# Reordering reciprocals, routed rows' normalisation and spare products in a one-core decoder layer

## What is computed

```
x = layernorm(x + attn(x))            # sparse attention: each token picks 96 of its keys by top-k
x = layernorm(x + retention(x, ctx))  # 16 heads, decaying causal mask
x = layernorm(x + moe(x))             # 8 experts, 2 chosen per token, gates from a softmax
```

## Time and profile before

| | us |
|---|---|
| median of three executions | 669.03 |
| the three | 668.65, 669.03, 680.7 |
| the profiled execution | 668.53 |
| its span, first to last instruction | 666.7 |

### The profile page before, as it was taken

How to read it: one execution, slowest core, us unless ns; L and a number is a source line. 1 busy time by engine, 2 the same in 40 slices (tenths; PEclk the granted TensorE clock), 3 DMA queues, 4 the chain that set the end, 5 groups by cost and what they waited for, 6 DMA issues and landing times.

```text
span 666.7 us, 22154 instructions
## 1 busy us (share of the span) xinstructions
PE 585.0 (88%) x8225; PEld 439.7 (66%) x8225; DVE 432.2 (65%) x1618; ACT 406.9 (61%) x1381; POOL 268.0 (40%) x428
## 2 busy tenths in 40 slices
PE   5478988998898699999999898989997997789996
PEld 4244664665566367867787577757775677778886
DVE  0938848865976777578657976478657775333653
ACT  4437756674776657668765676377755665445352
POOL 1413912911570497017502898219304652005310
PEclk9869999999999969999999899799999999799999
DMA  5030153122014051543353435344262623886551
GB/s 170 2 123 14 28 189 133 22 63 84 19 24 137 14 162 27 188 157 108 107 156 117 130 80 174 99 154 116 66 206 77 189 67 100 242 241 196 166 160 44
DMA packets 58594, 75.86 MB, mean 114 GB/s; under 512 B 14256, under 2 KB 47480, under 8 KB 57336
## 3 DMA queue, kind: packets, MB, share of 16 engines
q1 hardware_dynamic: 56952, 71.30, 35.8%
q0 software_dynamic: 1536, 3.15, 1.6%
HBM read 58.92 MB, written 8.62 MB: 101 GB/s over the span
## 4 chain that ended last, share of the span: by engine, by line
PE 34%; POOL 11%; issue 9%; ACT 6%; DVE 4%; DMA 1%; SPq 0%; DVEq 0%; POOLq 0%; ACTq 0%
PE bW L1364 4%; PE bH L1299 3%; PE bR L1314 3%; PE bG L1083 3%; PE bM L920 3%; POOL gb L852 3%; PE bH L1350 2%; PE bG L1350 2%; ACT qV L1567 2%; PE bS L1102 2%; PE bM L1130 1%; PE bR L1222 1%; PE bM L1125 1%; POOL sorted_tokens L864 1%; POOL acc L895 1%
## 5 line engine op out<-in xcount | busy, mean ns | idle before, releaser
L1515 ACT ACTIVATE ppn<-pp,rls 128x224 f32<-128x224 f32 (+1 forms) x128 | 59.0, 461 | 34.0 <-DVE rls L1815 33.7
L1833 DVE TENSOR_TENSOR gs<-bG,rank_t 96x512 f32<-96x512 f32 x96 | 65.5, 682 | 15.0 <-PE bG L1083 13.8
L1507 ACT ACTIVATE pp<-pp,nmx 128x224 f32<-128x224 f32 x96 | 46.5, 484 | 31.1 <-DVE nmx L1826 30.2
L1896 DVE TENSOR_TENSOR sm<-bC,cst 128x512 f32<-128x512 f32 x64 | 43.6, 681 | 23.0 <-PE bC L1239 23.0
L1083 PE MATMUL bG<-oh,kspl 128*96 128x512 f32 x160 | 56.6, 435 | 0.0
L810 POOL TENSOR_TENSOR r<-x,cst 128x256 f32<-128x256 f32 x8 | 5.8, 725 | 123.0 <-DVE x L1860 123.0
L1826 DVE CUSTOM_DVE_ANT_0 pp<-bS,cst 128x224 f32<-128x224 f32 x96 | 36.3, 378 | 27.3 <-PE bS L1102 27.2
L1599 ACT ACTIVATE ht<-bH,wt 128x128 f32<-128x128 f32 x156 | 44.4, 370 | 14.5 <-PE bH L1299 14.5
L920 PE MATMUL bM<-cst,ppn 128*128 128x128 f32 (+1 forms) x224 | 47.8, 284 | 5.5 <-ACT ppn L1515 5.3
L1525 ACT COPY pts<-bM 128x256 f32<-128x256 f32 x96 | 35.4, 369 | 27.2 <-PE bM L920 26.3
L1299 PE MATMUL bH<-xt,wt 128*128 128x128 f32 x312 | 43.5, 284 | 3.0 <-DVE xt L2025 3.0
(11 more groups left out here) (296 smaller groups left out, 1644.8 us busy)
## 6 DMA issues: line engine op xcount, KB each, us to landing
wt<-in_experts SPq DMA_DIRECT2D x61, 578.0 KB, 4.0
sidx<-far_slots SPq DMA_DIRECT2D x8, 1536.0 KB, 6.9
vstk<-gs SPq DMA_DIRECT2D x96, 64.0 KB
xs<-sorted_tokens SPq DMA_DIRECT2D x45, 64.0 KB, 3.9
expert_rows<-ot SPq DMA_DIRECT2D x45, 64.0 KB, 3.7
sorted_tokens<-acc SPq DMA_DIRECT2D x9, 256.0 KB, 2.9
cst<-shape_constants SPq DMA_DIRECT2D x1, 1595.5 KB, 6.3
xn<-in_x SPq DMA_DIRECT2D x8, 128.0 KB, 3.3
```

What stands on the lines that cost most here:

```text
L1507: AC(pp[:, s % 2, 0:w], bS[:, 0:w] if s < T0 else pp[:, s % 2, :], ACT.Exp, scale=1.0 if s < T0 else -1.0, bias=nmx[:, s % 2:s % 2 + 1], a ...
L1515: AC(ppn[:, t % 2, 0:w], pp[:, t % 2, 0:w], ACT.Copy, scale=rls[:, t % 2:t % 2 + 1]).then_inc(s_nrm.sem, 1)
L1833: TT(gs[:, g % 2, :].rearrange("p (t j) -> p t j", j=FAR), bG[0:96, :].rearrange("p (t j) -> p t j", j=FAR), rank_t[:, :].rearrange("p (o ...
L1896: free(TT(sm[:, u % 4, :].rearrange("p (v c) -> p v c", v=4), bC[:, :].rearrange("p (v c) -> p v c", v=4), C("causal").rearrange("p (o c) ...
```

## The change

It has three parts.

1. VectorE's reciprocal of tiles 3 to 15 moves from s+0.75 to s+0.25, ahead of the one-hot rows and of whatever stage C has at s+0.5. Tiles 0 to 2 keep their place. ScalarE's order is not touched.
2. The parts of the routed rows of batches 0 to 3 come earlier, by other tables. `collect` of the second batch of each group moves from slot 10 to 9, `summed` from slots 11 and 14 to 10 and 12, `means` from 14 and 17 to 13 and 15, and `normed` from 16 and 19 to 14 and 16.
3. Batch 0 has fewer fills: one product in slot 0 and one in slot 2 in place of two each in slots 0, 1 and 2. The other batches keep theirs (38 products in all before, 34 after).

```diff
+FILLS_FIRST, FILLS = 1, 2
 FETCH_SLOTS = (4, 5, 6)
-SUM_LATE, MEAN_LATE, NORM_LATE = 4, 7, 9
+SUM_LATE, MEAN_LATE, NORM_LATE = 3, 6, 7
...
             step, s = ends[g]
-            s += 2 + 3 * (n - GROUPS[g][0][0])
+            s += 2 + 2 * (n - GROUPS[g][0][0])
...
-                    if s in FILLED[i.n <= GROUPS[0][0][-1] + 1]:
-                        fill(2)
+                    if s in FILLED[0 < i.n <= GROUPS[0][0][-1] + 1]:
+                        fill(FILLS_FIRST if i.first else FILLS)
...
                     if s == 0:
-                        fill(2)
+                        fill(FILLS_FIRST if i.first else FILLS)
...
+            def inverse(i, t):
+
+                dve.wait_ge(s_exp.sem, s_exp.at(i.n, t + 1))
+                nc.vector.reciprocal(rls[:, t % 2:t % 2 + 1], lsum[:, t % 2:t % 2 + 1]).then_inc(s_rec.sem, 1)
+
             def stage_b(s, i):
                 p = i.par
                 if s < 0:
                     return
+                if s == int(s) + 0.25 and T0 - 1 <= s < NT:
+                    inverse(i, int(s))
                 if s in (1.25, 3.25, 5.25, 7.25, 9.25, 11.25):
...
-                if s == int(s) + 0.75 and s < NT:
-
-                    t = int(s)
-                    dve.wait_ge(s_exp.sem, s_exp.at(i.n, t + 1))
-                    nc.vector.reciprocal(rls[:, t % 2:t % 2 + 1], lsum[:, t % 2:t % 2 + 1]).then_inc(s_rec.sem, 1)
+                if s == int(s) + 0.75 and s < T0 - 1:
+                    inverse(i, int(s))
```

## The result

Side by side on one chip the changed kernel takes 675.27 us (median of 4, 672.37 to 677.1) against 668.84 before: a ratio of 1.011, with a 95% interval of 1.006 to 1.016. One of the four executions before, at 680.7 us, was a slow one and is left out of the ratio. The forecast was 667.2 us with a range of 660 to 673.5. The changed kernel is slower by 1%, under the 2% that I took as what a measurement can tell, but clear of its interval, and outside the range.

A forecast was written before the change was run, and what follows sets the result against it. TensorE, busy 88%, was taken as the bound, so edits count where it idles. Terms +5.9 - 5.0 + 0.7 - 2.5 = -0.9 us on 668.5 gave 667.6, stated as 667.2 us; own range 664 to 671, overall 660 to 673.5.

The forecast's parts named there:

- Part 1: Earlier reciprocals: VectorE's stands in slots 3, 7 and 15, less a gain, net +5.9 us, at most 8.3.
- waits for `ppn`: TensorE's waits, 5.3 us in all, mostly tile 2's: 1.2 us to be gained at tiles 5, 9 and 12.
- Slot 3: VectorE stands 0.98 us, some 0.35 returns a slot later: about 0.65 in five batches, 3.2 us.
- Slots 7 and 15: Slot 7: 0.46 us in batches 1, 2, 3, 5, total 1.8; slot 15: 0.75 in batches 0 to 2, total 2.1.
- VectorE's waits for the exponential: Sign for the reciprocals: VectorE's waits for ScalarE's exponential, called small now, rise to some 15 us.
- Part 2, step 7 to 8: Start of step 8: first product 3.4 us earlier, clock 1.6 us more; sum -5.0, ends -3.4 and -6.1.
- Part 2, step 5: End of step 5: late `acc` and `rkn` delay +2.0, `rqn` wait of 1.28 goes; net +0.7, ends -1.3 and +5.
- Part 3: Batch 0: fewer fills give 4.5 us at most, a later grant rise costs 2.0; net -2.5, ends -4.5 and +5.2.
- rival 3: Batch 0: the clock stays low without the fills, +5.2 us there; time 675.3 us; chance 0.10.
- rival 2: Slots 3, 7, 15 of every batch: VectorE's stands not given back, 8.3 to 12.7 us; 671 to 674.4 us; chance 0.14.
- Rival 1: The earlier reciprocals cost nothing; time 659.7, or 658.6 with the clock's whole share, taken as 660 us; chance 0.24.
- rival 4: Step 8's start: weights' load and `xt` late for another reason, other parts cancel, nothing reaches the end; 668.5 us; chance 0.08.

The follow-up runs named there:

- the control: The kernel before, unchanged, run and profiled again on the chip where other runs were made: ratio 1.0015 (0.998 to 1.005).
- tile 3 alone: The kernel before with only tile 3's reciprocal moved early, tables and fills as before: ratio 1.011 (1.007 to 1.016).
- the new tables alone: The kernel before with only the routed rows' parts earlier, reciprocals and fills as before: ratio 0.9915 (0.989 to 0.994), again 0.9935 (0.990 to 0.997).
- run of step 7 alone: The kernel before with the routed rows' parts earlier for batches 2 and 3 only: ratio 0.992 (0.988 to 0.995).

## Why the prediction was wrong

**Part 1, the step that failed.** The prediction had +5.9 us with an upper end of 8.3; the trace shows +17.3 in stage B. The upper end was itself mis-added: without the 1.2 us of waits for `ppn` the stands sum to 7.1, and the 1.2 was added once more. The trace's figure is one pair of executions; three things make up the difference to the forecast.

- *The term that was not in the sum: the clock.* I priced each stand at full clock and took the sum of stands for the price. Taking every quarter where the grant was 1.00, from this trace or, where it fell, from one of the others, the stands come to 8.4 us: batch 0 0.9, batches 1 and 2 2.5 each, batch 4 1.7, batch 6 0.4, and batch 7 about 0.5, never seen wholly at 1.00. The remaining 9 us came in quarters with a lowered grant. Some 1.7 of them, in batch 5 from mask 4, the control has as well, so about 7 us are part 1's. I had counted the clock in parts 2 and 3, where the trace of before showed it low, and not in part 1, where it showed 1.00 at each stand that I priced. But a grant of 1.00 there was not a reserve: TensorE already stood 0.63 to 0.85 us in slot 15, and with 1.44 to 1.66 it fell in 12 cases of 21.
- *Slot 3 was too cheap.* VectorE's stand was right: 0.98 us forecast, 0.94 measured. The timeline of the changed kernel, slot 3 of batch 1, as in the earlier trace rows:

```profile
110.25 0.19 ACT L1508 ACTIVATION_READ_ACCUMULATOR pp<-bS,nmx 128x1 f32 x1
110.47 0.16 DVE L1797 RECIPROCAL rls<-lsum 128x1 f32<-128x1 f32 x1 [0.94 <-ACT pp L1508]
110.55 0.73 DVE L1814 TENSOR_SCALAR oh<-sidx,cst 128x1024 fp32r<-128x1024 bf16 x1
111.20 0.68 DVE L1901 TENSOR_TENSOR sm<-bC,cst 128x512 f32<-128x512 f32 x1
...
111.94 0.50 PE L1240 MATMUL bC<-qV,kS 128*128 128x512 f32 x1 [1.53 <-DVE sm L1901]
```

TensorE's wait rose from 0.47 to 1.53, all of the stand. I let 0.35 come back one slot later; with tile 3 alone 0.65 does come back, but only behind mask 4, and with tile 7 early as well nothing does (0.51 more instead of 0.65 less). A slack was spent twice. Where I counted 0.65 it was 1.0 in batches 1 and 2, 1.2 in batches 4 and 6 (in 6 the 1.25 us that part 2 gives hide it) and 1.4 in batch 7; in batches 3 and 5 of this trace it was nothing.

- *The gain set against the stands did not come.* I took off 1.2 us for TensorE's waits for `ppn`. They went from 5.3 to 4.9 us, and most of the rest sits at tile 2, as I had said.

Slots 7 and 15 were right where the clock held: 0.46 forecast and 0.51 to 0.57 measured, 0.75 forecast and 0.63 to 0.83 measured in batches 1 and 2 (0.3 in batch 0 of the changed kernel). In batches 4 and 6, which I held for covered, tile 7 costs 0.5 to 0.65 us and gives it back behind mask 8; in batches 3 and 5 the clock moves the quarter in the control too, and the 0.46 cannot be read. It was right that expert products cover slot 15 from batch 3 on. Slots 8 to 11 of batches 1 and 2 cost 0.3 a batch that was not forecast, behind the wait for mask 8. VectorE's waits for the exponential rose by 15.7 us; I had said that they would rise to some 15, as if there were none before, where there were 12.3.

**Part 2, step 7 to 8: right.** -5.0 forecast, -5.0 in the trace. TensorE's waits there and the window behind them, as in the earlier trace rows:

```profile
575.76 1.16 PE L1300 MATMUL bH<-xt,wt 128*128 128x128 f32 x8 [1.48 <-DVE xt L2030]
...
578.22 0.30 PE L921 MATMUL bC<-cst,rqn 128*128 128x128 f32 x1 [0.29 <-POOL rqn L816]
...
579.78 1.16 PE L1300 MATMUL bG<-xt,wt 128*128 128x128 f32 x8 [1.26 <-DVE xt L2030]
```

```profile
576.00:584.00 8.00, 5.82 (x48) 5.23 (x47) 2.36 (x6) 4.44 (x13) 1.99 (x4) 1.00 0.66 193
```

2.84, 1.82 and 1.83 have become 1.48, 0.29 and 1.26 (I said 1.5 and 1.4), there is no wait for `wt`, and the grant stays at 1.00. That it meets the forecast to a tenth is luck: the three other traces of the first kind with these tables gain 4.9, 4.4 and 2.9 us there, and on the second kind of chip the same stretch gains 2 to 4 us. The run of step 7 alone is 0.8% faster in time, of which its trace shows only 2.5 us at this place.

**Part 2, step 5: the sum nearly right, by terms that were not.** The wait for `rqn` of 1.28 us goes, as said: with the new tables alone the quarter from mask 0 of batch 6 is 1.25 us shorter. The delay of 2.0 us does not come. I held `acc` of batch 0 at the old time and let VectorE run into it, but the collect in front of it on GpSimd is one of the parts that moved. In before GpSimd starts the second collect at 402.95, 2.3 us behind mask 12:

```profile
402.95 0.98 POOL L852 DMA_INDIRECT gb<-expert_rows,slot  x1 [0.27 <-POOL kstk L801]
```

and in the changed kernel at 410.14, 4.6 us ahead of it (mask 12 is at 414.71); `acc` is ready at 417.84 and VectorE comes at 423.31:

```profile
410.14 0.98 POOL L853 DMA_INDIRECT gb<-expert_rows,slot  x1 [0.27 <-POOL kstk L802]
...
417.11 0.73 POOL L887 TENSOR_TENSOR acc<-acc,x 128x256 f32<-128x256 f32 x1
```

The -3.5 us that this trace shows at the place are the grant of the earlier trace rows that did not recur, not the change: the control has them too. The split of `rks`, which took 1.52 us in the earlier trace rows and which the prediction expected to stay that long beside GpSimd's normalisation, took 0.79 us beside it (GpSimd's L896 runs from 426.08 to 427.67):

```profile
427.07 0.79 DVE L1736 TENSOR_TENSOR rks<-rkn,high 128x512 uint32<-128x512 uint32 x1
```

So that expectation failed; what made the split long before is not shown.

**Part 3: near in the trace by luck, nothing in the time.** -2.5 forecast, -1.3 in the trace, no difference between the two kernels timed beside each other; the unchanged kernel's own two traces differ by 1.65 us in that quarter. That the grant would rise later was right (0.77 and 0.81 in place of 1.00 from 44 to 60).

**The rivals.** The measured 675.3 is rival 3's number and near rival 2's 671 to 674.4, by chance: the mechanism is neither's. Rival 2 had the place, VectorE's stands that are not given back, but reached its price by batches that were in fact covered. Rival 3 had the clock, but in batch 0, where the later rise cost less than the fills that went. What happened is rival 2's stand with rival 3's clock. Rival 1, reciprocals that cost nothing, is refuted, and so is rival 4, since the first product at the start of step 8 did come earlier.

## What to carry to other kernels

A stand added to an engine that feeds TensorE costs its length, and behind it the risk of a stretch at half the clock: here 0.3 to 0.8 us where the grant held, 2.1 to 3.3 where it fell, in more than half of the cases. Where such a stand cannot be avoided, a product of constants in it can keep the grant up: 1.02 us of it did in six quarters of six, at no cost that the quarters show. Slack that one edit is said to use up must be counted once over all edits; and before a low grant in one trace is counted as something to win back, the unchanged kernel should be profiled a second time.

## What was not expected of the hardware

This kernel takes 668 us on some chips and 687 on others. The control's span is 16.7 us longer than the first trace's, and 14.6 us of that lie between masks 4 and 8 of batch 7 (another 4.1, from mask 8 of batch 5, are outweighed by the quarters that the clock made shorter). There three engines stand at once, and GpSimd issues eight collects. Rows of the control, TensorE, ScalarE, GpSimd:

```profile
530.78 1.11 PE L1223 MATMUL bR<-sm,cnm 128*32 128x128 f32 x5 [0.80 <-issue]
...
535.12 1.09 PE L1223 MATMUL bR<-sm,cnm 128*32 128x128 f32 x4 [0.81 <-issue]
```

```profile
523.18 0.26 ACT L1524 COPY pts<-bM 96x128 f32<-96x128 f32 x1 [5.61 <-remote]
...
537.27 0.37 ACT L1526 COPY pts<-bM 128x256 f32<-128x256 f32 x1 [9.97 <-remote]
```

```profile
526.50 0.98 POOL L853 DMA_INDIRECT gb<-expert_rows,slot  x1 [4.80 <-DMA expert_rows<-ot]
...
535.29 0.94 POOL L853 DMA_INDIRECT gb<-expert_rows,slot  x1 [0.30 <-issue]
```

ScalarE stands 9.97 us, and TensorE halts between the groups of one product, on nothing that the trace names. In the first trace the same collects, from 523.28 on, leave ScalarE no wait above 1.5 us, each for a named releaser. The collects need not be the cause: ScalarE's wait of 5.61 us ends before the first of them is issued at 526.50. The low grant behind the stands is part of the price: TensorE is busy 20.56 us for the same 200 instructions in this quarter, at a mean grant of 0.56, where it was 12.40 at 0.87. What differs in the chips no run here shows.
